# Moving a bias add and PSUM evacuation from TensorE and ScalarE to VectorE, and splitting and merging transposing DMAs, in a linear-attention and ternary-FFN block

## The chip, the cores and the metric

One Trainium2 chip, eight cores. Each core runs the same program on one of eight sequences; nothing is exchanged between them. The metric is the device time of the slowest core in microseconds (us).

## The reference

Per sequence `x` is 4096 x 1024, float32. Attention is linear: no 4096 x 4096 matrix is formed.

```python
h   = layernorm(x)
qkv = h @ Wqkv + bqkv                  # 1024 -> 3072
q, k, v = split(qkv)
q = q / norm(q);  k = k / norm(k)
kv = sum over all rows of (k * v)      # one row of 1024
x = x + (q * kv) @ Wout + bout
h = layernorm(layernorm(x)) * g1 + b1l
h = gelu(h @ ternary(w1).T + b1)       # 1024 -> 4096
h = layernorm(h) * g2 + b2l
x = x + h @ ternary(w2).T + b2         # 4096 -> 1024
# ternary(w) = clip(round(w / m), -1, 1) * m,  m = mean |w|
```

`kv` needs every row before the first output row can be made, so the kernel has two stages.

## The kernel before

The engines' programs are written out by hand, each in one function (`sync`, `scalar`, `gpsimd`, `tensor`, `vector`), and meet only in semaphores. The order of work on an engine is the order of the code, and an instruction that waits holds up all that stands behind it on its engine. A tile is 128 rows; there are NT = 32 tiles.

**First stage** (`for j in range(NT)` in `scalar` and `vector`). SyncE loads tile j of x (L292). ScalarE and VectorE take sum and sum of squares together (`scA_front` L341, `dvA_front` L781); ScalarE writes the normalised tile in bf16 (L353) and stores it to DRAM (L358). SyncE reads it back transposed, eight DMAs of 128 x 128 a tile (`h1t_tile`, L281), into `h1T`, one tile later in the loop. TensorE computes qkv of a tile in six groups of 512 columns. Each group is one float32 matmul over a single row of ones, which puts the bias `rowsA` into the bank (L577, two instructions), and eight bf16 matmuls (L581). The groups take four PSUM banks `pq` in turn, so group i waits until group i-4 has been copied out.

Three tiles behind, `scA_back(u)` (L361) on ScalarE copies the six banks to `qkvb` (L370), squares and sums q and k (L373, L378), and writes `qhat` (L386, stored to DRAM at L390) and `khat` (L395). VectorE (`dvA_back`, L811) gives the two reciprocals (L814, L817), multiplies khat by v (L820) and adds to `kv_acc` (L823).

Beside this the weights w1 and w2 are read by GpSimd through a ring of five slots `wstg` (L539): first VectorE sums their absolute values, six blocks a tile (L770, in tiles 0 to 10 of the loop), then, from u = 10 to u = 25, ScalarE takes two signs of each of four blocks a tile (L427, L429, behind `khat`), VectorE adds them (L778), and GpSimd stores them (L528, L532).

**Between the stages** every engine meets at a barrier; the ternary weights are read back transposed (L308: 4096 rows each, L314: 1024 rows each), scaled and summed.

**Second stage** (pairs of tiles, `for p in range(NT // 2)`). TensorE: `attn_mm(t)` multiplies the transposed q, held in one buffer `qT`, with the scaled Wout (L660). SyncE fills `qT` with eight transposing DMAs a tile (L325), after `attn_mm` of the tile before has ended (semaphore `batt`). `dv_front` and `sc_front` normalise the sum (L935 to L964, L455 to L470), TensorE transposes it (L699), multiplies with w1 for two tiles at once (L719), ScalarE applies Gelu (L493), TensorE multiplies with w2 (L678), and `dv_tail` and `sc_tail` finish and store the tile (L1020 to L1028, L480). In a pair p with tiles j0 and j1, ScalarE runs: `sc_front(j0 + 2)`, 32 Gelus, `sc_tail(j0)`, `sc_front(j1 + 2)`, `sc_tail(j1)`. The w1 matmuls use two PSUM banks, so the third group waits for the first Gelu.

Of the kernel before, what the change touches and what calls it, by code (L numbers as in the profile page):

```python
# [9 lines left out]
F32 = mybir.dt.float32  # L10
BF16 = mybir.dt.bfloat16
AF = mybir.ActivationFunctionType
ALU = mybir.AluOpType
# [42 lines left out]
def build_program(T):  # L56
# [95 lines left out]
    wqkvp = sbA("wqkvp", [128, 8 * E3], BF16)  # L152
    xbufA = sbA("xbufA", [128, 2 * D], F32)
# [114 lines left out]
    with es, esB, psB, nc.Block() as block:  # L268

        @block.sync  # L270
        def _(sy):
            def h1t_tile(jt):
                gt = jt // 4
                st = jt % 4
                sy.wait_ge(ah1w.h(jt % 2), 16 * (jt // 2 + 1))
                if jt >= 4:
                    sy.wait_ge(ah1t.h(jt % 4), 128 * (jt // 4))
                if gt >= 2 and st == 0:
                    sy.wait_ge(aqkv.h, 24 * (gt - 1))
                for c in range(8):  # L280
                    ah1t.inc(sy.dma_start(  # L281
                        out=h1T[:, (gt % 2) * 4096 + c * 512 + st * 128:
                                (gt % 2) * 4096 + c * 512 + (st + 1) * 128],
                        in_=h1_d[jt * 128:(jt + 1) * 128, c * 128:(c + 1) * 128],
                        transpose=True), jt)

            for g in range(NG):
                for s in range(4):
# [6 lines left out]
                    if j - 2 >= 0:  # L295
                        h1t_tile(j - 2)
            for jt in (4 * NG - 2, 4 * NG - 1):
                h1t_tile(jt)
# [18 lines left out]
            for j in range(NT):  # L317
# [4 lines left out]
                if j >= 1:  # L322
                    sy.wait_ge(batt.h, 2 * j)
                for c in range(8):
                    bqt.inc(sy.dma_start(  # L325
                        out=qT[:, c * 128:(c + 1) * 128],
                        in_=qh_d[j * 128:(j + 1) * 128, c * 128:(c + 1) * 128],
                        transpose=True), 16)
# [3 lines left out]
        def _(sc):  # L332
# [28 lines left out]
            def scA_back(u):  # L361
                P = (u % 2) * 16
                if u >= 1:
                    sc.wait_ge(akv.h, u)
                for e in range(6):
                    i = u * 6 + e
                    sc.wait_ge(aqkv.h, i + 1)
                    if e == 0 and u >= 1:
                        sc.wait_ge(aqh.h, u)
                    aevac.inc(sc.activation(out=qkvb[:, e * 512:(e + 1) * 512],  # L370
                                            in_=pq[i % 4][:, :], func=AF.Copy))
                sc.drain()
# [4 lines left out]
                                      in_=stA[:, P + 8:P + 9], func=AF.Sqrt))  # L377
                sc.activation(out=sqscrA[:, :], in_=qkvb[:, D:2 * D],  # L378
# [70 lines left out]

            def sc_front(t):  # L450
# [31 lines left out]

# [645 lines left out]
```

## Time and profile before

| | us |
|---|---|
| median of two runs | 2851.97 |
| the two runs | 2849.68, 2854.25 |
| the profiled execution | 2851.01 |
| its span on the slowest core (core 5) | 2849.4 |
| spans of the eight cores | 2828.0 to 2849.4 |
| mean granted TensorE clock, core 5 | 0.825 of full |
| TensorE / VectorE / ScalarE busy over the span | 67% / 31% / 31% |

The span runs from the first to the last instruction of a core. Busy shares are means over two stages that differ much, so they are of little use alone; the stages are read apart. The granted clock is the share of full speed that the chip allowed TensorE; it moves between 0.5 (1.2 GHz) and 1.0 (2.4 GHz).

### The profile page before, as it was taken

How to read it: one execution, taken by the hardware profiler on the slowest of the kernel's cores; microseconds unless marked ns; L12 is line 12 of the kernel's file. 1: busy time of each engine (PE TensorE's matmuls, PEld its weight loads, DVE VectorE, ACT ScalarE, POOL GpSimd, SP SyncE). 2: the span in 40 equal slices, each digit the busy share in tenths (PEclk: the TensorE clock that was granted, in tenths of full speed). 3: DMA queues.
4: the chain of work that ended last, by engine and by line, in shares of the span. 5: the costliest groups of instructions: out<-in, count | busy, mean ns of one | idle time of the engine just before them, and what ended most of it. 6: DMA issues, size and time to landing. Idle time of an engine off the chain costs nothing.

```text
span 2849.4 us, 36124 instructions; the slowest of 8 cores (2828.0 to 2849.4 us)
## 1 busy us (share of the span) xinstructions
PE 1910.8 (67%) x11300; PEld 960.2 (34%) x11300; DVE 889.3 (31%) x2504; ACT 874.0 (31%) x1505; POOL 118.0 (4%) x217
## 2 busy tenths in 40 slices
PE   0467786666566691457767867686776678677767
PEld 0122221222122230215534544453454345344434
DVE  0533322222222211232253234224323522433343
ACT  0233345655555441002312221321222132212311
POOL 2110001111111000000000000000000000000000
PEclk9977787777766695568889989888998889899889
DMA  9854324444434306700010010001001000100000
GB/s 134 236 166 139 131 67 130 126 129 129 137 123 122 92 30 121 137 23 19 31 38 20 23 34 25 27 26 37 20 23 34 29 28 22 35 20 23 27 16 16
DMA packets 203597, 195.44 MB, mean 69 GB/s; under 512 B 160404, under 2 KB 160405, under 8 KB 203415
## 3 DMA queue, kind: packets, MB, share of 16 engines
q0 software_dynamic: 31200, 92.34, 11.9%
q1 hardware_dynamic: 157952, 67.18, 10.0%
q10 hardware_dynamic: 14264, 33.62, 3.2%
q8 instruction: 100, 1.64, 0.2%
q14 instruction: 81, 0.66, 0.1%
HBM read 117.55 MB, written 50.33 MB: 59 GB/s over the span
## 4 chain that ended last, share of the span: by engine, by line
PE 50%; DVE 12%; ACT 11%; issue 8%; DVEq 7%; DMA 5%; SPq 4%; ACTq 2%; POOL 1%; POOLq 0%
PE py L678 17%; PE py L719 16%; PE pqkv L581 7%; PE pqkv L577 4%; DMA wstg<-w 4%; PE patt L660 2%; DVEq L936 2%; DVEq L790 2%; SPq L314 2%; DVE wpart L770 2%; SPq L308 1%; DVE z1T L1036 1%; DVE outbuf L1020 1%; DVEq L1027 1%; DVE xring L941 1%
## 5 line engine op out<-in xcount | busy, mean ns | idle before, releaser
L678 PE MATMUL py<-w2p,h4buf 128*128 128x512 bf16 x2048 | 541.6, 399 | 124.9 <-DVE outbuf L1028 123.7
L719 PE MATMUL py<-z1T,w1p 128*128 128x256 bf16 x4096 | 481.8, 281 | 165.4 <-ACT h4buf L493 163.6
L577 PE MATMUL pqkv<-rowsA,onesrow 1*128 1x512 f32 x384 | 263.9, 772 | 363.1 <-ACT qkvb L370 284.5
L719 PEld LDWEIGHTS py<-z1T,w1p 128*128 128x128 bf16 x4096 | 382.9, 100 | 264.9 <-issue 170.6
L581 PE MATMUL pqkv<-wqkvp,h1T 128*128 128x512 bf16 x1536 | 448.9, 445 | 0.0
L978 DVE TENSOR_TENSOR h4sq<-h4buf 128x128 bf16<-128x128 bf16 x1024 | 223.3, 225 | 292.5 <-PE psumSQ L687 259.9
L493 ACT ACTIVATE h4buf<-py,beta1c 128x256 bf16<-128x256 f32 x512 | 241.1, 474 | 229.8 <-PE py L719 229.1
L581 PEld LDWEIGHTS pqkv<-wqkvp,h1T 128*128 128x128 bf16 x1536 | 151.6, 109 | 367.4 <-issue 267.5
L1036 DVE CAST z1T<-pzT 128x128 bf16<-128x128 f32 x256 | 56.6, 284 | 580.7 <-PE pzT L699 580.7
L687 PE MATMUL psumSQ<-onesb,h4sq 128*128 128x1 bf16 x1024 | 167.4, 163 | 85.3 <-DVE h4sq L978 85.3
L577 PEld LDWEIGHTS pqkv<-rowsA,onesrow 1*128 1x128 f32 x384 | 68.3, 221 | 462.5 <-issue 462.5
L370 ACT ACTIVATE qkvb<-pqkv 128x512 f32<-128x512 f32 x192 | 104.6, 600 | 274.5 <-PE pqkv L581 246.6
L687 PEld LDWEIGHTS psumSQ<-onesb,h4sq 128*128 128x128 bf16 x1024 | 102.8, 100 | 227.1 <-issue 118.3
L684 PE MATMUL psumSQ<-onesb,h4buf 128*128 128x1 bf16 x1024 | 173.4, 169 | 0.0
L678 PEld LDWEIGHTS py<-w2p,h4buf 128*128 128x128 bf16 x2048 | 125.1, 96 | 128.8 <-issue 127.9
L814 DVE RECIPROCAL stA<-stA 128x1 f32<-128x1 f32 x32 | 5.3, 164 | 463.4 <-ACT stA L376 463.4
L684 PEld LDWEIGHTS psumSQ<-onesb,h4buf 128*128 128x128 bf16 x1024 | 103.3, 101 | 138.2 <-issue 27.8
L455 ACT ACTIVATE xbufB<-xring 128x512 f32<-128x512 f32 x32 | 20.1, 629 | 401.2 <-DVE xring L941 401.2
L660 PE MATMUL patt<-woutp,qT 128*128 128x512 bf16 x512 | 122.3, 394 | 15.9 <-DMA qT<-qhscr 15.9
L477 ACT ACT_TABLE_LOAD x16 | 20.5, 1283 | 355.4 <-DVE stB L1005 355.4
L477 ACT ACTIVATE stB<-stB 128x1 f32<-128x1 f32 x32 | 6.5, 203 | 327.1 <-DVE stB L1005 327.0
L539 POOL DMA_DIRECT2D wstg<-w x128 | 67.7, 530 | 275.1 <-DVE wpart L770 274.3
(124 smaller groups left out, 1370.7 us busy)
## 6 DMA issues: line engine op xcount, KB each, us to landing
wstg<-w POOLq DMA_DIRECT2D x128, 512.0 KB, 5.7
xbufA<-x SPq DMA_DIRECT2D x32, 512.0 KB, 5.2
xbufB<-x SPq DMA_DIRECT2D x32, 512.0 KB, 3.5
out<-outbuf ACTq DMA_DIRECT2D x32, 512.0 KB, 2.7
h1scr<-h1buf ACTq DMA_DIRECT2D x32, 256.0 KB, 5.4
qhscr<-qhat ACTq DMA_DIRECT2D x32, 256.0 KB, 2.0
wqkvp<-wqkv POOLq DMA_DIRECT2D x8, 768.0 KB, 26.1
h1T<-h1scr SPq DMA_TRANSPOSE x256, 2.4
```

Source lines behind the costliest of these rows:

```text
L370: aevac.inc(sc.activation(out=qkvb[:, e * 512:(e + 1) * 512], in_=pq[i % 4][:, :], func=AF.Copy))
L493: bh4.inc(sc.activation(out=h4buf[:, m * 256:(m + 1) * 256], in_=py1[m % 2][:, :], func=AF.Gelu, bias=beta1c[:, m:m + 1]))
L539: wld.inc(gp.dma_start(out=wslot(i), in_=w_src(kind, ch)), i)
L577: te.matmul(out=pq[i % 4][:, :], lhsT=onesrow[:, :], rhs=rowsA[0:1, e * 512:(e + 1) * 512], start=True, stop=False)
L581: mm = te.matmul(out=pq[i % 4][:, :], lhsT=h1T[:, (g % 2) * 4096 + c * 512 + s * 128: (g % 2) * 4096 + c * 512 + (s + 1) * 128], rhs=wqkvp ...
L660: mm = te.matmul(out=patt[:, hh * 512:(hh + 1) * 512], lhsT=qT[:, c * 128:(c + 1) * 128], rhs=woutp[:, c * D + hh * 512:c * D + (hh + 1) * ...
L678: mm = te.matmul(out=py2[:, hh * 512:(hh + 1) * 512], lhsT=h4m, rhs=w2p[:, m * D + hh * 512:m * D + (hh + 1) * 512], start=(m == 0), stop= ...
L684: te.matmul(out=psumSQ[:, m:m + 1], lhsT=h4m, rhs=onesb[:, :], start=True, stop=True)
L687: bsq4.inc(te.matmul(out=psumSQ[:, 32 + m:33 + m], lhsT=h4sq[:, (m % 4) * 128:(m % 4 + 1) * 128], rhs=onesb[:, :], start=True, stop=True))
L719: mm = te.matmul(out=py1[m % 2][:, :], lhsT=w1p[:, c * H + m * 128:c * H + (m + 1) * 128], rhs=z1T[:, c * 256:(c + 1) * 256], start=(c == ...
L978: bsq.inc(dv.tensor_tensor(out=h4sq[:, (m % 4) * 128:(m % 4 + 1) * 128], in0=h4m, in1=h4m, op=ALU.mult))
L1036: cp = dv.tensor_copy(out=z1T[:, c * 256 + (t % 2) * 128:c * 256 + (t % 2) * 128 + 128], in_=pzT[:, cc * 128:(cc + 1) * 128])
```

## The change

It has four parts.

- The bias is added elsewhere. The 192 bias matmuls in the loop go. Before the loop TensorE broadcasts the bias once over 128 partitions, in six pieces through two banks, and VectorE copies it to a new tensor `bqkvb`.
- The six copies out of PSUM go from ScalarE to VectorE, as additions of the bank and `bqkvb`, ahead of the reciprocals in `dvA_back`. ScalarE squares q once two of them are done, and k once four are.
- `h1T` is filled two tiles at a time, with eight DMAs of 256 x 128 in the odd iterations, instead of eight of 128 x 128 in each.
- The `qT` transposes of the odd tiles are issued by ScalarE (`qt_issue`) and no longer by SyncE: that of tile 1 ahead of the second stage's loop, that of tile j1 + 2 at the head of pair p.

```diff
+    bqkvb = sbA("bqkvb", [128, E3], F32)
...
-            def h1t_tile(jt):
+            def h1t_half(jt):
                 gt = jt // 4
                 st = jt % 4
-                sy.wait_ge(ah1w.h(jt % 2), 16 * (jt // 2 + 1))
-                if jt >= 4:
-                    sy.wait_ge(ah1t.h(jt % 4), 128 * (jt // 4))
+                hg = jt // 2
+                sy.wait_ge(ah1w.h(0), 16 * (jt // 2 + 1))
+                sy.wait_ge(ah1w.h(1), 16 * (jt // 2 + 1))
+                if hg >= 4:
+                    sy.wait_ge(ah1t.h(hg % 4), 128 * (hg // 4))
                 if gt >= 2 and st == 0:
                     sy.wait_ge(aqkv.h, 24 * (gt - 1))
                 for c in range(8):
                     ah1t.inc(sy.dma_start(
                         out=h1T[:, (gt % 2) * 4096 + c * 512 + st * 128:
-                                (gt % 2) * 4096 + c * 512 + (st + 1) * 128],
-                        in_=h1_d[jt * 128:(jt + 1) * 128, c * 128:(c + 1) * 128],
-                        transpose=True), jt)
+                                (gt % 2) * 4096 + c * 512 + (st + 2) * 128],
+                        in_=h1_d[jt * 128:(jt + 2) * 128, c * 128:(c + 1) * 128],
+                        transpose=True), hg)
...
-                    if j - 2 >= 0:
-                        h1t_tile(j - 2)
-            for jt in (4 * NG - 2, 4 * NG - 1):
-                h1t_tile(jt)
+                    if j >= 3 and j % 2 == 1:
+                        h1t_half(j - 3)
+            h1t_half(4 * NG - 2)
...
-                if j >= 1:
-                    sy.wait_ge(batt.h, 2 * j)
-                for c in range(8):
-                    bqt.inc(sy.dma_start(
-                        out=qT[:, c * 128:(c + 1) * 128],
-                        in_=qh_d[j * 128:(j + 1) * 128, c * 128:(c + 1) * 128],
-                        transpose=True), 16)
+                if j % 2 == 0:
+                    if j >= 1:
+                        sy.wait_ge(batt.h, 2 * j)
+                    for c in range(8):
+                        bqt.inc(sy.dma_start(
+                            out=qT[:, c * 128:(c + 1) * 128],
+                            in_=qh_d[j * 128:(j + 1) * 128, c * 128:(c + 1) * 128],
+                            transpose=True), 16)
...
             def scA_back(u):
                 P = (u % 2) * 16
-                if u >= 1:
-                    sc.wait_ge(akv.h, u)
-                for e in range(6):
-                    i = u * 6 + e
-                    sc.wait_ge(aqkv.h, i + 1)
-                    if e == 0 and u >= 1:
-                        sc.wait_ge(aqh.h, u)
-                    aevac.inc(sc.activation(out=qkvb[:, e * 512:(e + 1) * 512],
-                                            in_=pq[i % 4][:, :], func=AF.Copy))
-                sc.drain()
+                sc.wait_ge(aevac.h, 6 * u + 2)
                 sc.activation(out=sqscrA[:, :], in_=qkvb[:, 0:D], func=AF.Square,
                               accum_out=stA[:, P + 8:P + 9])
                 sc.drain()
                 aqs.inc(sc.activation(out=stA[:, P + 9:P + 10],
                                       in_=stA[:, P + 8:P + 9], func=AF.Sqrt))
+                sc.wait_ge(aevac.h, 6 * u + 4)
                 sc.activation(out=sqscrA[:, :], in_=qkvb[:, D:2 * D],
                               func=AF.Square, accum_out=stA[:, P + 10:P + 11])
...
+            def qt_issue(t):
+                sc.wait_ge(batt.h, 2 * t)
+                for c in range(8):
+                    bqt.inc(sc.dma_start(
+                        out=qT[:, c * 128:(c + 1) * 128],
+                        in_=qh_d[t * 128:(t + 1) * 128, c * 128:(c + 1) * 128],
+                        transpose=True), 16)
...
+            qt_issue(1)
             sc_front(0)
             sc_front(1)
             for p in range(NT // 2):
                 j0, j1 = 2 * p, 2 * p + 1
+                if j1 + 2 < NT:
+                    qt_issue(j1 + 2)
                 if j0 + 2 < NT:
                     sc_front(j0 + 2)
...
+            for e in range(6):
+                if e >= 2:
+                    te.wait_ge(binit.h, e - 1)
+                abc.inc(te.matmul(out=pq[e % 2][:, :], lhsT=onesrow[:, :],
+                                  rhs=rowsA[0:1, e * 512:(e + 1) * 512],
+                                  start=True, stop=True))
             for hh in range(2):
+                te.wait_ge(binit.h, 5 + hh)
...
-            te.wait_ge(binit.h, 2)
+            te.wait_ge(binit.h, 8)
...
-                    te.wait_ge(ah1t.h(s), 128 * (g + 1))
+                    hg = 2 * g + s // 2
+                    te.wait_ge(ah1t.h(hg % 4), 128 * (hg // 4 + 1))
                     for e in range(6):
                         i = (4 * g + s) * 6 + e
                         if i >= 4:
                             te.wait_ge(aevac.h, i - 3)
-                        te.matmul(out=pq[i % 4][:, :], lhsT=onesrow[:, :],
-                                  rhs=rowsA[0:1, e * 512:(e + 1) * 512],
-                                  start=True, stop=False)
...
-                                start=False, stop=(c == 7))
+                                start=(c == 0), stop=(c == 7))
...
+            for e in range(6):
+                dv.wait_ge(abc.h, e + 1)
+                binit.inc(dv.tensor_copy(out=bqkvb[:, e * 512:(e + 1) * 512],
+                                         in_=pq[e % 2][:, :]))
...
             def dvA_back(u):
                 P = (u % 2) * 16
+                for e in range(6):
+                    i = u * 6 + e
+                    dv.wait_ge(aqkv.h, i + 1)
+                    if e == 0 and u >= 1:
+                        dv.wait_ge(aqh.h, u)
+                    if e == 2 and u >= 1:
+                        dv.wait_ge(akh.h, u)
+                    aevac.inc(dv.tensor_tensor(
+                        out=qkvb[:, e * 512:(e + 1) * 512],
+                        in0=pq[i % 4][:, :],
+                        in1=bqkvb[:, e * 512:(e + 1) * 512], op=ALU.add))
                 dv.wait_ge(aqs.h, u + 1)
```

Unchanged: what is computed, the order of tiles, the weights' path, and the second stage but for who issues the odd `qT`.

VectorE in the first stage, one tile of the part that makes ternary weights; before:

```order
L808 TENSOR_TENSOR stA<-stA 128x1
L814 RECIPROCAL stA<-stA 128x1
L817 RECIPROCAL stA<-stA 128x1
L820 TENSOR_TENSOR kvtmp<-khat,qkvb 128x1024
L823 TENSOR_TENSOR kv_acc<-kv_acc,kvtmp 128x1024
L778 TENSOR_TENSOR qod<-qod,qog 128x1024 x2
L778 TENSOR_TENSOR qtd<-qtd,qtg 128x1024 x2
L788 TENSOR_REDUCE stA<-xbufA 128x1
L791 TENSOR_SCALAR stA<-stA 128x1
```

and after:

```order
L823 TENSOR_TENSOR stA<-stA 128x1
L835 TENSOR_TENSOR qkvb<-pqkv,bqkvb 128x512 x6
L840 RECIPROCAL stA<-stA 128x1
L843 RECIPROCAL stA<-stA 128x1
L846 TENSOR_TENSOR kvtmp<-khat,qkvb 128x1024
L849 TENSOR_TENSOR kv_acc<-kv_acc,kvtmp 128x1024
L793 TENSOR_TENSOR qod<-qod,qog 128x1024 x2
L793 TENSOR_TENSOR qtd<-qtd,qtg 128x1024 x2
L803 TENSOR_REDUCE stA<-xbufA 128x1
L806 TENSOR_SCALAR stA<-stA 128x1
```

Six additions from the banks `pqkv` now stand between the last small operation of the front (a row that writes `stA`) and the two reciprocals; the signs' sums (`qod`, `qtd`) and the next tile's `TENSOR_REDUCE` stay behind `kv_acc`.

ScalarE in the second stage, from the end of one pair to the first Gelus of the next (`out` is the store of a finished tile, the operations on `xbufB` are the squares of `sc_front`); before:

```order
L477 ACTIVATE stB<-stB 128x1
L480 DMA out<-outbuf 128x1024
L455 ACTIVATE xbufB,stB<-xring 128x512
L457 ACTIVATE xbufB,stB<-xring 128x512
L460 ACTIVATE stB<-stB 128x1
L465 ACTIVATE stB<-stB 128x1
L470 ACTIVATE z1buf<-xring,stB 128x1024
L493 ACTIVATE h4buf<-py_0,beta1c 128x256
```

and after:

```order
L480 ACTIVATE stB<-stB 128x1
L483 DMA out<-outbuf 128x1024
L448 DMA_TRANSPOSE qT<-qhscr 128x128 x8
L458 ACTIVATE xbufB,stB<-xring 128x512
L460 ACTIVATE xbufB,stB<-xring 128x512
L463 ACTIVATE stB<-stB 128x1
L468 ACTIVATE stB<-stB 128x1
L473 ACTIVATE z1buf<-xring,stB 128x1024
L499 ACTIVATE h4buf<-py_0,beta1c 128x256
```

Eight transposing DMAs now stand between the store and the squares of the next front.

## Rows read from the trace of the kernel before

**Rows 1.** Windows of core 5: us, busy (x) of each engine, PEclk, DMA share, GB/s.

```profile
412.00:970.00 558.00, 359.68 (x964) 113.87 (x964) 120.75 (x246) 315.96 (x417) 66.93 (x125) 0.72 0.41 125
1241.00:2849.00 1608.00, 1165.51 (x8961) 712.73 (x8960) 578.76 (x1922) 386.99 (x800) 0.00 (x0) 0.87 0.09 26
```

**Rows 2.** Timeline of ScalarE at four tiles: start, us, engine, line, form.

```profile
119.54 1.24 ACT L353 ACTIVATE h1buf<-xbufA,stA 128x1024 bf16<-128x1024 f32 x1 [0.65 <-DVE stA L808]
...
362.62 1.24 ACT L353 ACTIVATE h1buf<-xbufA,stA 128x1024 bf16<-128x1024 f32 x1 [0.65 <-DVE stA L808]
...
411.79 1.24 ACT L353 ACTIVATE h1buf<-xbufA,stA 128x1024 bf16<-128x1024 f32 x1 [0.65 <-DVE stA L808]
...
969.83 1.24 ACT L353 ACTIVATE h1buf<-xbufA,stA 128x1024 bf16<-128x1024 f32 x1 [0.65 <-DVE stA L808]
```

**Rows 3.** The line of the last accumulation: ns min/median/max, first and last start.

```profile
L823 DVE TENSOR_TENSOR kv_acc<-kv_acc,kvtmp x32: 1225/1226/1226, 137.1 to 1086.5; 128x1024 f32<-128x1024 f32 x32
```

**Rows 4.** Timeline, 548 to 584 us: one tile of the ternary stretch.

```profile
548.17 2.07 ACT L370 ACTIVATE qkvb<-pqkv 128x512 f32<-128x512 f32 x4 [0.66 <-ACT h1buf L353]
...
548.91 2.04 PE L577 MATMUL pqkv<-rowsA,onesrow 1*128 1x512 f32 x2 [12.17 <-ACT qkvb L370]
550.88 3.59 PE L581 MATMUL pqkv<-wqkvp,h1T 128*128 128x512 bf16 x8
...
554.57 0.60 ACT L370 ACTIVATE qkvb<-pqkv 128x512 f32<-128x512 f32 x1 [4.34 <-PE pqkv L581]
...
560.10 0.60 ACT L370 ACTIVATE qkvb<-pqkv 128x512 f32<-128x512 f32 x1 [4.93 <-PE pqkv L581]
...
563.93 1.90 PE L581 MATMUL pqkv<-wqkvp,h1T 128*128 128x512 bf16 x8
...
565.17 1.15 ACT L395 ACTIVATE khat<-qkvb,stA 128x1024 f32<-128x1024 f32 x1 [0.57 <-ACT qhat L386]
...
578.06 1.21 DVE L788 TENSOR_REDUCE stA<-xbufA 128x1 f32<-128x1024 f32 x1
...
580.71 0.16 DVE L808 TENSOR_TENSOR stA<-stA 128x1 f32<-128x1 f32 x1
...
582.92 1.57 ACT L370 ACTIVATE qkvb<-pqkv 128x512 f32<-128x512 f32 x3 [0.66 <-ACT h1buf L353]
```

**Rows 5.** Timeline, 195 to 232 us: one tile of the stretch that sums weights.

```profile
200.12 6.84 DVE L770 TENSOR_REDUCE wpart<-wstg 128x1 f32<-128x1024 f32 x6
...
206.87 1.22 DVE L788 TENSOR_REDUCE stA<-xbufA 128x1 f32<-128x1024 f32 x1
...
211.74 2.06 ACT L370 ACTIVATE qkvb<-pqkv 128x512 f32<-128x512 f32 x4 [0.66 <-ACT h1buf L353]
...
221.40 0.60 ACT L370 ACTIVATE qkvb<-pqkv 128x512 f32<-128x512 f32 x1 [2.66 <-PE pqkv L581]
```

**Rows 6.** Timeline, 22 to 77 us: the bias of the output projection at the start.

```profile
22.35 3.75 PE L565 MATMUL pqkv<-boutrow,onesrow 1*128 1x512 f32 x4 [22.35 <-DMA identb<-ident_d]
...
75.43 1.28 DVE L748 COPY boutb<-pqkv 128x512 f32<-128x512 f32 x2
```

**Rows 7.** Timeline, 1677 to 1690 us: the start of a pair in the second stage.

```profile
1677.32 9.92 SPq L325 DMA_TRANSPOSE qT<-qhscr  x8
...
1680.51 0.34 ACTq L480 DMA_DIRECT2D out<-outbuf  x1
...
1683.16 0.63 ACT L455 ACTIVATE xbufB<-xring 128x512 f32<-128x512 f32 x1 [7.22 <-DVE xring L941]
...
1689.71 3.57 PE L719 MATMUL py<-z1T,w1p 128*128 128x256 bf16 x16 [10.71 <-ACT h4buf L493]
```

**Rows 8.** Three DMA issuing lines: ns min/median/max, first and last start.

```profile
L314 SPq DMA_TRANSPOSE w2p<-wq2scr x32: 1144/1273/3143, 1138.8 to 1185.1; - x32
L325 SPq DMA_TRANSPOSE qT<-qhscr x256: 1085/1202/2376, 1187.0 to 2676.0; - x128
L390 ACTq DMA_DIRECT2D qhscr<-qhat x32: 338/338/367, 134.1 to 1083.5; - x32
```

More of the change, by code:

```diff
@@ L745, in _ @@
                                       scalar1=0.5, scalar2=None, op0=ALU.mult))
+            for e in range(6):
+                dv.wait_ge(abc.h, e + 1)
+                binit.inc(dv.tensor_copy(out=bqkvb[:, e * 512:(e + 1) * 512],
+                                         in_=pq[e % 2][:, :]))
             for hh in range(2):
-                dv.wait_ge(abc.h, hh + 1)
+                dv.wait_ge(abc.h, 7 + hh)
                 binit.inc(dv.tensor_copy(out=boutb[:, hh * 512:(hh + 1) * 512],
@@ L1069, in build_program @@
         "mpre": 2, "mtot": 2, "mval": 2, "mbc": 2, "m1r": 1, "m2r": 1,
-        "abc": 2, "binit": 2, "kvc": 8, "kvw": 1, "bar": 5,
+        "abc": 8, "binit": 8, "kvc": 8, "kvw": 1, "bar": 5,
         "w1t": 128, "w2t": 512,
@@ L1080, in build_program @@
     }
-    dexpect = {"ax": 16 * NT, "ah1w": 16 * NT, "ah1t": 512 * NG,
+    dexpect = {"ax": 16 * NT, "ah1w": 16 * NT, "ah1t": 64 * NT,
                "aqw": 16 * NT, "wld": 16 * NLOADS,
```

## The prediction

> **What bounds the kernel now.** I read the stages apart: first the windows, then the timeline of single tiles inside them. TensorE is granted 0.72 of its clock and works 359.68 of 558 us in the stretch that makes ternary weights, and 1165.51 of 1608 us in the second stage [rows 1]. So it bounds neither stage alone: something makes it wait once a tile and once a pair, and the chain through that wait sets the time.
>
> In the first stage the start of `h1buf` on ScalarE marks the tiles. From 119.54 to 362.62 eight intervals sum weights (30.4 us each), two up to 411.79 do neither (24.6 us), sixteen up to 969.83 make ternary weights (34.9 us), and the last accumulation starts at 1086.5 and ends 1.2 later [rows 2, 3], 117.9 us after 969.83. One tile of the ternary stretch shows the loop [rows 4]. ScalarE copies four banks at 548.17 that had long been full. TensorE waited 12.17 us for the first of them, and then does two groups at the low clock, 2.04 of bias and about 3.5 of real work each. ScalarE waits 4.34 and 4.93 us for them and ends its sixth copy at 560.70. Only then come the squares, qhat and khat (to 566.32), eight signs, and the next front. The loop is ScalarE and VectorE in series with two groups of TensorE, nothing of which overlaps.
>
> The second stage's 1608 us hold 16 pairs, about 100 each [rows 1]. At its start TensorE has two w1 groups done and waits 10.71 us for the first Gelu, which stands behind `sc_front` on ScalarE [rows 7]. `sc_front` itself starts at 1683.16, after VectorE has finished the old tile and made the new sum. The transposes of the odd q tile run meanwhile on SyncE, from 1677.32 for 9.92 us, and hold nobody up.
>
> **First stage, the loop.** I count from r, the start of VectorE's reduction of the front. Before, the ternary tile's r is 578.06, its first copy starts at r + 4.9 and ends its sixth 12.5 later (560.70 less 548.17), at r + 17.4; khat ends 5.6 after that, at r + 23.0 [rows 4]. After, VectorE is free when the front's last operation ends, at 580.87, r + 2.8, and need not wait for h1buf. One addition of 128 x 512 float32 out of PSUM isn't in the trace. Half of one of 128 x 1024 is 0.61 us [rows 3], and the copies of a bank at the start take 0.64 each [rows 6]; I take 0.65, nearer to the row with PSUM (both ends together move a tile by 0.1). The first ends at r + 3.55 and frees TensorE. Its group is now only the eight matmuls, 3.59 us at the low clock [rows 4], so the fifth group ends at r + 7.1 and the sixth, if still slow, at r + 10.7; the sixth addition ends at r + 11.4. The squares run on ScalarE under this. VectorE's reciprocals stand behind all six additions: the new wait costs ScalarE some 3 us of idleness ahead of qhat. After 0.35 us for both, qhat, the issue of its store and khat take 1.15 + 0.57 + 1.15, and khat ends at r + 14.6. That is 8.4 earlier. The rest of the tile stays as it is, signs included. The ring of weights must turn faster; at a DMA share of 0.41 [rows 1] I give back 0.3. **Sixteen tiles by 8.1: -130 us.** If the sixth group runs at the high clock (1.90 [rows 4]) it is 27 us more.
>
> For the tiles that sum weights r is 206.87, the first copy starts at r + 4.9 and the sixth ends at 222.0, r + 15.1, with khat 5.6 on at r + 20.7 [rows 5]. There only one group ran slow. New: 3.55 + 3.59 + 1.90 + 0.65 = r + 9.7, khat at r + 12.9, 7.8 earlier. The six sums of 6.84 us [rows 5] then ask for six blocks in about 23 us instead of 30, so I give back 0.8. **Eight tiles by 7.0: -56.** The two tiles without weights end at khat's 12.9 plus two operations of 1.23 [rows 3], near 16 each instead of 24.6: **-17.** From 969.83 on there are two such intervals (32), a back alone (13), and three tiles without a front. Those three were TensorE's: six groups with their bias. Now six by 1.90 is 11.4, and I take 12 each. 32 + 13 + 36 = 81 against 117.9: **-37.**
>
> The removed bias matmuls are thus worth 2 us a slow group where VectorE waits for it, and the moved copies the time that ScalarE stood behind h1buf and its store. I don't add TensorE's whole bias time, since most of it lay in the shade of the signs.
>
> **Merged transposes.** A DMA of 1024 rows occupies SyncE 1273 ns, one of 128 rows 1202 [rows 8], so one of 256 costs about 1.2, and SyncE issues half as many. But SyncE is not in the loop: gain nothing. An even tile's `h1T` now comes with the odd one: behind the odd tile's h1buf lie its store, eight issues of 1.2, 9.6 us, and two landings. TensorE asks for it one interval later plus two groups, near 20 us even at 16 us a tile. The cover is thin in the short tiles, and worth 2 to 4 us each if gone. At the very start it makes TensorE's first group later by about one interval of the start and its eight issues, of which nearly all lies beside the first three fronts.
>
> **Start.** Six more banks are broadcast and copied. VectorE reaches them only at 75.43 [rows 6]. Two are ready by then; six more follow at 1.9 each (half of 3.75 [rows 6]), about 12 us on VectorE's path. The transfers that keep VectorE waiting afterwards get ahead meanwhile, so from 0 to 14 I take **+10**, near the upper end, as the later h1T is in it.
>
> **Second stage.** The eight issues stand on ScalarE now, behind the store (issued at 1680.51, done at 1680.85 [rows 7]) and before `sc_front`. Behind them are queued the squares, the root, z1buf, and all 32 Gelus; VectorE waits for the squares and TensorE for the Gelus. The trace has no transpose on ScalarE. SyncE's row has 1202 ns each, 9.92 us for eight; a plain store issued on ScalarE has 338 ns, so eight would be 2.7 [rows 7, 8]. Those are the ends, and I take 9.92, the same operation on the same kind of queue. `sc_front` then starts at 1690.8 instead of 1683.16, 7.6 later; at the lower end 0.4. The wait for `attn_mm` (done at 1677.3) is over before. All of it is on the path, since TensorE already waits for that very Gelu and has nothing else in its program. No gain stands against it, since SyncE's transposes were hidden. Fourteen pairs by 7.6 and the first, where no store or tail hides anything, by 8.6: **+115 us.** The last pair has none.
>
> The Trainium skill (DMA: Bandwidth & Descriptors, "Issuing engines are not separate DMA queues") says that spreading DMAs over engines saves only the sequencer's issue time, usually small beside the transfer. Taken as a price for ScalarE, that would make this part nearly free; the 1202 ns of the row speak against it here, and no run yet shows it on ScalarE. The same skill (TensorE: Matmul & The Clock Gate, on queue depths) calls ScalarE's queue strictly first in, first out, which is why I let the Gelus wait.
>
> **Sum.** -130 - 56 - 17 - 37 + 10 + 115 = -115. The profiled execution took 2851.0 us, span 2849.4; that gives 2736. The median of the runs is 1 us above the profiled one: **2737 us.**
>
> **Rivals.**
> - *Issuing a transpose on ScalarE is as cheap as a store.* Then the second stage loses 0.4 by 15, 6 us and not 115: 2737 - 109 = 2628. For it: the stores' 338 ns. Against: the same operation's 1202 on SyncE. This is also where the page's rule leads. Chance 0.08.
> - *Half of the loop's gain goes into a new wait*: the ring of weights or a late `h1T` becomes what ends last. For it: the DMA share of 0.41, and bursts of six blocks through five slots. Half of 240 is 120: 2857. Chance 0.13.
> - *The weight stream paces the stage wholly.* If GpSimd's ring cannot turn faster than 30.4 and 34.9 us, the 24 weight tiles gain nothing. What is left is -54, against +125: 2923, slower. It decides where those tiles gain less than 3.0 us each (71 by 24). Against: [rows 5] shows six blocks consumed in 6.84 us with no gap, so they had landed early. Chance 0.06.
> - *TensorE's clock.* Its wait per pair grows from 10.7 to 18.3 us. After 10.71 the first sixteen w1 matmuls take 3.57 instead of about 1.9 [rows 7]. If a longer wait left the clock low for one more such stretch, 1.7 to 3.5 us by 15 would be added: 2763 to 2790. It lies inside the forecast's case.
>
> **How the numbers follow.** The forecast's case gets 0.73. Its own range is 2680 to 2795: down by the fast sixth group (27), issues of 1.085 (17) and a free start (10), up by the clock (52) and the start. A measurement of this kernel tells about 2%, 57 us, from no change. Faster by more than that (under 2795) are the forecast's case and the first rival: 0.80. Within 2% is mostly the second: 0.14. Slower by over 2% is the third: 0.06. The range leaves out most of the first and third and part of the second: 2665 to 2840.
>
> **What would show it.** Right: no `rowsA` matmul in the loop; additions near 0.65; h1buf intervals of about 23, 16 and 27 us; ScalarE idle before qhat for VectorE's reciprocal; an ACTq row of eight transposes near 9.8 us at the head of each pair, and TensorE idle some 18 us before the w1 matmuls, in pairs 7 to 8 us longer. Wrong: transposes of 0.35 on ScalarE, or squares that start beside them; intervals above 30 with VectorE or ScalarE waiting for `wstg`; TensorE waiting for `h1T`.

## The result, and the profile after

The changed kernel takes 2781.32 us (median of 11 runs, 2773.42 to 2787.67), in a ratio of 0.973 to the kernel before run beside it (ten runs, median 2857.46), 95% interval 0.9701 to 0.9759: faster by 2.7%. Here and below medians are over all runs of a kernel and ratios are not: in some runs the cores of one die show a lower clock and a longer span, and those stand outside the ratios. The profiled execution took 2781.41, its span on core 6 is 2779.9 against 2849.4 before. The direction and the range held; the point, 2737, was 44 us low.

The end of the first stage (the last accumulation) parts the span in two. Before it comes at 1087.7 us, now at 864.7. What follows took 1761.7 us and now takes 1915.1. So the first stage gave 223.0 us and the second took 153.4 back.

The marks of the first stage, that answer to [rows 2, 3]: the starts of `h1buf` on ScalarE in tiles 3, 11, 13 and 29 (columns: start, us, engine, line, form), in the changed kernel.

```profile
132.44 1.24 ACT L356 ACTIVATE h1buf<-xbufA,stA 128x1024 bf16<-128x1024 f32 x1 [0.65 <-DVE stA L823]
...
335.10 1.24 ACT L356 ACTIVATE h1buf<-xbufA,stA 128x1024 bf16<-128x1024 f32 x1 [0.65 <-DVE stA L823]
...
367.82 1.24 ACT L356 ACTIVATE h1buf<-xbufA,stA 128x1024 bf16<-128x1024 f32 x1 [0.65 <-DVE stA L823]
...
788.32 1.24 ACT L356 ACTIVATE h1buf<-xbufA,stA 128x1024 bf16<-128x1024 f32 x1 [0.65 <-DVE stA L823]
```

And the line of `kv_acc`, whose last instruction ends the stage (duration ns min/median/max, first and last start):

```profile
L849 DVE TENSOR_TENSOR kv_acc<-kv_acc,kvtmp x32: 1224/1226/1226, 159.4 to 863.5; 128x1024 f32<-128x1024 f32 x32
```

The sixteen ternary tiles now take 26.3 us each, (788.32 - 367.82) / 16, instead of 34.9. One of them, answering to [rows 4], in the timeline of the changed kernel:

```profile
495.54 1.21 DVE L803 TENSOR_REDUCE stA<-xbufA 128x1 f32<-128x1024 f32 x1
...
498.72 2.48 DVE L835 TENSOR_TENSOR qkvb<-pqkv,bqkvb 128x512 f32<-128x512 f32 x4
498.86 1.24 ACT L356 ACTIVATE h1buf<-xbufA,stA 128x1024 bf16<-128x1024 f32 x1 [0.65 <-DVE stA L823]
499.56 5.86 PE L592 MATMUL pqkv<-wqkvp,h1T 128*128 128x512 bf16 x16 [13.78 <-DVE qkvb L835]
...
503.24 0.69 DVE L835 TENSOR_TENSOR qkvb<-pqkv,bqkvb 128x512 f32<-128x512 f32 x1 [2.03 <-PE pqkv L592]
...
505.52 0.69 DVE L835 TENSOR_TENSOR qkvb<-pqkv,bqkvb 128x512 f32<-128x512 f32 x1 [1.59 <-PE pqkv L592]
...
506.44 1.15 ACT L381 ACTIVATE qhat<-qkvb,stA 128x1024 bf16<-128x1024 f32 x1 [3.06 <-DVE stA L840]
508.16 1.15 ACT L390 ACTIVATE khat<-qkvb,stA 128x1024 f32<-128x1024 f32 x1 [0.57 <-ACT qhat L381]
...
520.83 1.21 DVE L803 TENSOR_REDUCE stA<-xbufA 128x1 f32<-128x1024 f32 x1
```

Counted from r, the start of VectorE's `TENSOR_REDUCE`, its additions start at r + 3.2 (498.72 less 495.54), beside ScalarE's h1buf and no longer behind it. TensorE's two groups take 5.86 us together and not 11 (the granted clock is 0.50 up to 503.20 and 0.80 in the 2.3 us after it, so the second group is partly fast). The sixth addition ends at r + 10.7. ScalarE then has waited 3.06 us for the reciprocal, and khat ends at r + 13.8; before it was r + 23.0.

At the head of a pair of the second stage, answering to [rows 7]:

```profile
1607.81 0.34 ACTq L483 DMA_DIRECT2D out<-outbuf  x1
1608.23 10.29 ACTq L448 DMA_TRANSPOSE qT<-qhscr  x8
...
1618.62 0.63 ACT L458 ACTIVATE xbufB<-xring 128x512 f32<-128x512 f32 x1 [15.38 <-issue]
...
1625.17 7.02 PE L730 MATMUL py<-z1T,w1p 128*128 128x256 bf16 x39 [18.88 <-ACT h4buf L499]
```

(The last row counts only what had started when the window asked for ended.) The eight issues hold ScalarE for 10.29 us. The first square starts 10.81 us after the store, where it was 2.65 (1683.16 less 1680.51). TensorE waits 18.88 us, where it was 10.71. The pairs, from first Gelu to first Gelu, take 109.2 us in the mean of fourteen and not 99.0.

Behind the wait TensorE runs slower too. Two groups by line (busy us, mean ns of one, idle before and its releaser), first of the kernel before, then of the changed one:

```profile
L678 PE MATMUL py<-w2p,h4buf 128*128 128x512 bf16 x2048 | 541.6, 399 | 124.9 <-DVE outbuf L1028 123.7
L719 PE MATMUL py<-z1T,w1p 128*128 128x256 bf16 x4096 | 481.8, 281 | 165.4 <-ACT h4buf L493 163.6 <-DVE z1T L1036 1.4
```

```profile
L689 PE MATMUL py<-w2p,h4buf 128*128 128x512 bf16 x2048 | 560.0, 409 | 125.4 <-DVE outbuf L1054 124.2 <-issue 0.2
L730 PE MATMUL py<-z1T,w1p 128*128 128x256 bf16 x4096 | 494.1, 286 | 287.3 <-ACT h4buf L499 285.8 <-DVE z1T L1062 1.4
```

The same 2048 and 4096 matmuls take 30.7 us more (560.0 + 494.1 against 541.6 + 481.8), 2.0 a pair, and the wait for the Gelu 122.2 us more (285.8 against 163.6), 8.1 in each of fifteen pairs. Together 152.9 of the 153.4 us, 10.2 a pair.

### The profile page after: what moved, and what is told of

The parts are those of the page before. It is cut to its first block, busy times and chain, and to the rows that moved or that the text cites. A ratio compares the mean times of both kernels' runs of the same rounds, so it can differ in the third digit from the quotient of the medians.

```text
span 2779.9 us, 35286 instructions; the slowest of 8 cores (2757.0 to 2779.9 us)
## 1 busy us (share of the span) xinstructions
PE 1660.3 (60%) x10928; PEld 917.9 (33%) x10928; DVE 1011.1 (36%) x2702; ACT 771.0 (28%) x1313; POOL 118.0 (4%) x217
## 4 chain that ended last, share of the span: by engine, by line
PE 48%; DVE 12%; issue 9%; ACT 8%; ACTq 7%; DMA 6%; DVEq 6%; SPq 4%; POOL 1%; POOLq 0%
PE py L689 18%; PE py L730 17%; PE pqkv L592 7%; ACTq L448 6%; DMA wstg<-w 4%; PE patt L671 2%; DVEq L805 2%; SPq L316 2%; DVE z1T L1062 1%; SPq L310 1%; DVE outbuf L1046 1%; DVEq L1053 1%; DVE kvtmp L846 1%; ACT qhat L381 1%; ACT khat L390 1%
## 5 line engine op out<-in xcount | busy, mean ns | idle before, releaser
L730 PE MATMUL py<-z1T,w1p 128*128 128x256 bf16 x4096 | 494.1, 286 | 287.3 <-ACT h4buf L499 285.8
L689 PE MATMUL py<-w2p,h4buf 128*128 128x512 bf16 x2048 | 560.0, 409 | 125.4 <-DVE outbuf L1054 124.2
L592 PE MATMUL pqkv<-wqkvp,h1T 128*128 128x512 bf16 x1536 | 397.7, 426 | 371.5 <-DVE qkvb L835 318.3
L730 PEld LDWEIGHTS py<-z1T,w1p 128*128 128x128 bf16 x4096 | 390.4, 102 | 391.6 <-issue 292.0
L592 PEld LDWEIGHTS pqkv<-wqkvp,h1T 128*128 128x128 bf16 x1536 | 162.1, 107 | 606.3 <-issue 468.2
L835 DVE TENSOR_TENSOR qkvb<-pqkv,bqkvb 128x512 f32<-128x512 f32 x192 | 124.1, 687 | 120.5 <-PE pqkv L592 119.7
L785 DVE TENSOR_REDUCE wpart<-wstg 128x1 f32<-128x1024 f32 x64 | 74.5, 1214 | 16.7 <-DMA wstg<-w 16.4
L671 PEld LDWEIGHTS patt<-woutp,qT 128*128 128x128 bf16 x512 | 50.4, 101 | 75.0 <-issue 24.2
L846 DVE TENSOR_TENSOR kvtmp<-khat,qkvb 128x1024 f32<-128x1024 f32 x32 | 39.2, 1226 | 98.7 <-ACT khat L390 98.7
```

The lines of the kernel that those rows point to most:

```text
L592: mm = te.matmul(out=pq[i % 4][:, :], lhsT=h1T[:, (g % 2) * 4096 + c * 512 + s * 128: (g % 2) * 4096 + c * 512 + (s + 1) * 128], rhs=wqkvp ...
L671: mm = te.matmul(out=patt[:, hh * 512:(hh + 1) * 512], lhsT=qT[:, c * 128:(c + 1) * 128], rhs=woutp[:, c * D + hh * 512:c * D + (hh + 1) * ...
L689: mm = te.matmul(out=py2[:, hh * 512:(hh + 1) * 512], lhsT=h4m, rhs=w2p[:, m * D + hh * 512:m * D + (hh + 1) * 512], start=(m == 0), stop= ...
L730: mm = te.matmul(out=py1[m % 2][:, :], lhsT=w1p[:, c * H + m * 128:c * H + (m + 1) * 128], rhs=z1T[:, c * 256:(c + 1) * 256], start=(c == ...
L785: dcons.inc(dv.tensor_reduce(out=wpart[:, col:col + 1], in_=wslot(i), axis=AX.X, op=ALU.add, apply_absolute_value=True))
L835: aevac.inc(dv.tensor_tensor(out=qkvb[:, e * 512:(e + 1) * 512], in0=pq[i % 4][:, :], in1=bqkvb[:, e * 512:(e + 1) * 512], op=ALU.add))
```

## The experiments

Every run is compared with runs of the kernel before on its own chip; those had medians of 2863, 2865 and 2856 us in the three groups (e1 to e4, e5 to e8, f1 to f3), so across groups only ratios are set side by side. "End of first stage" is the end of the last accumulation, on the slowest core.

### e1: all qT transposes back on SyncE

```diff
-                if j % 2 == 0:
-                    if j >= 1:
-                        sy.wait_ge(batt.h, 2 * j)
...
+                if j >= 1:
+                    sy.wait_ge(batt.h, 2 * j)
...
-            qt_issue(1)
...
-                if j1 + 2 < NT:
-                    qt_issue(j1 + 2)
```

> The changed kernel with all qT transposes back on SyncE. Theory: the eight issues on ScalarE are the whole loss of the second stage, in two parts: the wait for the first Gelu (7.4 us a pair) and about 2.8 us a pair of low TensorE clock behind it. Without them the pair returns from 109.2 to 99.0 us, and the kernel comes to 2781 - 15 x 10.2 = 2628 us. Rival: the longer pairs belong to the clock after another first stage, or to the loads of x; then only the 15 x 7.4 of the wait comes back: 2670 us, with pairs near 102.

2640.7 us, ratio 0.9205 (0.9153 to 0.9258). Pairs are 99.0 us again, and what follows the first stage takes 1765.7. The matmuls behind the wait are back too:

```profile
L677 PE MATMUL py<-w2p,h4buf 128*128 128x512 bf16 x2048 | 542.1, 399 | 125.5 <-DVE outbuf L1042 124.2 <-issue 0.2
L718 PE MATMUL py<-z1T,w1p 128*128 128x256 bf16 x4096 | 481.9, 281 | 164.8 <-ACT h4buf L487 163.1 <-DVE z1T L1050 1.3
```

542.1 and 481.9 are the numbers of before. So both the wait and the slow matmuls hang on the moved issues, and the one edit costs 0.973 - 0.9205 of the time before, 5.3% or 150 us. The theory's 2628 was reckoned from the first runs, beside which the kernel before took 2857 us; here it takes 2863.

### e2: only the moved qT transposes

```diff
 (kernel before)
+                if j % 2 == 0:
+                    if j >= 1:
+                        sy.wait_ge(batt.h, 2 * j)
...
+            qt_issue(1)
...
+                if j1 + 2 < NT:
+                    qt_issue(j1 + 2)
```

> The kernel before with only the odd qT transposes moved to ScalarE. Theory: plus 15 x 10.2 = 153 us, so about 3005 us, pairs of 109.2 us, first stage as before. Rival (parts depend on each other): under 2980, or a first stage that changes too.

3017.3 us, ratio 1.0515 (1.0459 to 1.0571), pairs of 109.2; the first stage ends at 1096.5, with ternary tiles of 34.7. The loss is the same beside the old first stage, 5.2%: the parts add up.

### e3: only the bias and PSUM part

```diff
 (changed kernel, h1t_tile and qT on SyncE as before)
```

> The kernel before with only the bias and PSUM part: neither the merged transposes nor the moved qT. Theory: the whole gain of the first stage is here, and the merged transposes only cost: their even tile comes late at the start. First h1T at about 115 us instead of 141, and 10 to 15 us faster than the kernel with all qT on SyncE: about 2615 us. Rival: the merged transposes relieve SyncE and the DMA queues and carry a part of the gain; then this is slower than that kernel, above 2635.

2635.0 us, ratio 0.9175 (0.9097 to 0.9253). The first stage ends at 871.9, ternary tiles take 27.3, and TensorE's first group starts at 120.5 us. The whole gain is in this part. That it is also faster than e1 by the cost of the merged transposes isn't settled: 0.9175 and 0.9205 lie inside each other's intervals.

### e4: only the merged h1T transposes

```diff
 (kernel before)
-                    if j - 2 >= 0:
-                        h1t_tile(j - 2)
+                    if j >= 3 and j % 2 == 1:
+                        h1t_half(j - 3)
...
```

> The kernel before with only the merged h1T transposes. Theory: SyncE isn't in the loop, so nothing is gained; the first tile is late and costs 5 to 15 us once: 2857 to 2867 us. Rival: half as many transposes free DMA time for the weights: 10 us or more faster than before, under 2842.

2877.3 us, ratio 1.0044 (1.0018 to 1.0071): 13 us slower. The first wait of TensorE shows it, from the waits of this run and of the one before it (engine, line, releaser: us, times, longest):

```profile
PE pqkv L579 <- DMA h1T<-h1scr: 106.2, 1, 106.2
```

```profile
PE pqkv L578 <- DMA h1T<-h1scr: 30.6, 1, 30.6
```

The first tile's `h1T` is waited for 106.2 us, against 78.5 in the kernel before; in e3 it is 30.6 after the bias broadcasts. So the wait is 28 us longer, of which 13 reach the end. Ternary tiles are as long as before (34.9). The merging gains nothing, and what it costs arises at the start.

### e5: the bias matmuls back on TensorE

```diff
+                        te.matmul(out=pq[i % 4][:, :], lhsT=onesrow[:, :],
+                                  rhs=rowsA[0:1, e * 512:(e + 1) * 512],
+                                  start=True, stop=False)
...
-                    aevac.inc(dv.tensor_tensor(
+                    aevac.inc(dv.tensor_copy(
```

> The run with the bias and PSUM part alone, but the bias matmuls put back in front of each group and VectorE only copying the bank (the broadcast before the loop stays). It parts the two gains. Theory: of the ternary tile's 7.6 us the bias's share is the two slow groups, 2 x 2.0 us, and the move's share 3.5 to 4: tiles of 31 us in the ternary stretch, 26 in the sums', and the last tiles back at 17.3; in all about 16 x 3.8 + 8 x 3 + 2 x 3 + 25 = 115 us slower than that run, near 2750. Rival: only the move counts, since the matmuls lie in the shade of the signs: under 2680.

2764.5 us, ratio 0.9631 (0.9589 to 0.9673), so beside e3 (0.9175, with an interval of 0.8% to either side) the bias matmuls are worth some 4.6% and the move alone 3.7%. The first stage ends at 993.0. Ternary tiles take 30.8 us, tiles that sum weights 26.8, those with neither 20.8, and from tile 29 to the end 104.8 instead of 75.2. Two slow groups of one tile, from its timeline:

```profile
578.01 2.04 PE L577 MATMUL pqkv<-rowsA,onesrow 1*128 1x512 f32 x2 [7.63 <-DVE qkvb L824]
...
579.98 3.59 PE L581 MATMUL pqkv<-wqkvp,h1T 128*128 128x512 bf16 x8
...
583.50 2.07 PE L577 MATMUL pqkv<-rowsA,onesrow 1*128 1x512 f32 x2
...
585.51 3.59 PE L581 MATMUL pqkv<-wqkvp,h1T 128*128 128x512 bf16 x8
...
589.21 0.69 DVE L824 COPY qkvb<-pqkv 128x512 f32<-128x512 f32 x1 [4.83 <-PE pqkv L581]
```

Each group has 2.0 us of bias in front of VectorE's copy. The gain is thus about half one and half the other in the ternary tiles (34.9, 30.8, 27.3), and two thirds bias from tile 29 on (29.6 of 42.7 us).

### e6: the reciprocals ahead of the sixth addition

```diff
+                    if e == 4:
+                        dv.wait_ge(aqs.h, u + 1)
+                        aqr.inc(dv.reciprocal(...))
+                        dv.wait_ge(aks.h, u + 1)
+                        akr.inc(dv.reciprocal(...))
+                dv.wait_ge(aevac.h, 6 * (u + 1))
```

> The run with the bias and PSUM part alone, with both reciprocals ahead of the sixth addition. Theory: ScalarE's wait before qhat (2 to 3 us in the trace) is the place of the reciprocals in VectorE's program; qhat and khat move up by one group of TensorE and an addition (2.4 to 3.6 us), so tiles with signs are 2.5 to 3 us shorter, those that end on VectorE 1 to 1.5: about 55 us faster, 2580. Rival: the gain goes into a wait for the weights' landings or the sixth group: under 20 us.

2565.0 us, ratio 0.8941 (0.8903 to 0.8979), 2.3% less than e3's. Ternary tiles are 24.8 us, those that sum weights 21.6, those with neither 13.4. ScalarE's wait before qhat, in the waits of e3 and of this run:

```profile
ACT qhat L379 <- DVE stA L826: 92.9, 32, 3.8
```

```profile
ACT qhat L379 <- DVE stA L827: 20.7, 29, 1.1
```

92.9 us became 20.7. The place of two operations of 0.15 us behind an addition that waits for TensorE had cost 1.8 to 3.1 us in each tile.

### e7: TensorE kept busy in the wait, in the changed kernel

```diff
+                    if m == 2:
+                        for _ in range(150):
+                            te.matmul(out=pzT[:, 0:256], lhsT=w1p[:, 0:128],
+                                      rhs=z1T[:, 0:256], start=True, stop=True)
```

> The changed kernel with 150 additional 256-column matmuls into a free bank while TensorE waits for the first Gelu of a pair (extra work whose result nobody reads). Theory: the 2.8 us a pair beyond the wait are the clock, which falls in a wait of 19 us and costs again behind it. With the array busy it stays at full: pairs of 104.5 to 106.5 us instead of 109.2, 40 to 70 us faster, 2711 to 2741. Rival: the clock isn't the cause, or falls elsewhere: pairs of 109 or more.

2778.3 us, ratio 0.9683 (0.9651 to 0.9715), against 0.973 (0.9701 to 0.9759): not told apart. Pairs scatter from 105.2 to 109.3 us, 107.7 in the mean where they were 109.2, and the mean granted clock rose from 0.807 to 0.858 on the slowest core. The expected 104.5 to 106.5 was missed, but not because the clock doesn't matter:

```profile
L689 PE MATMUL py<-w2p,h4buf 128*128 128x512 bf16 x2048 | 551.7, 404 | 125.1 <-DVE outbuf L1058 124.3
L734 PE MATMUL py<-z1T,w1p 128*128 128x256 bf16 x4096 | 469.1, 277 | 44.4 <-ACT h4buf L499 42.9 <-DVE z1T L1066 1.4
L729 PE MATMUL pzT<-z1T,w1p 128*128 128x256 bf16 x2400 | 265.3, 273 | 0.0
```

The real matmuls take 33.3 us less than in the changed kernel (551.7 + 469.1 against 560.0 + 494.1). The added ones and what is left of the wait take 22.4 more than the wait did (265.3 + 42.9 against 285.8); the last pair has no long wait to fill, and from its first Gelu to the end takes 88.3 us and not 78.2. Behind the first stage this profile has 1893.3 us where the changed kernel has 1915.1; its first stage, which the edit doesn't touch, was longer (to 885.7 and not 864.7). So most of what filling gave back it also cost.

### e8: eight plain stores in place of the transposes

```diff
 (e1's kernel)
+                sc.wait_ge(batt.h, 2 * t)
+                for c in range(8):
+                    bdum.inc(sc.dma_start(out=dum_d[c * 128:(c + 1) * 128, :],
+                                          in_=boutb[:, 0:1]), 16)
```

> The changed kernel with all qT transposes on SyncE, and at the place on ScalarE where the odd ones stood eight plain stores of 512 bytes each to a scratch tensor. It prices the rival of my prediction. Theory: the cost is the time that an issue holds ScalarE. Eight plain ones are 8 x 0.34 = 2.7 us, of which all but 0.4 lies beside VectorE's own chain: pairs of 99.0 to 99.6, within 10 us of the run without them (2641). Rival: any eight DMAs there cost the same as transposes: pairs of 106 or more.

2706.93 us in the one run that could be compared; no ratio was worked out. The profile is of another (2753.6), and the timeline is of core 4, whose span is 2680.9 us, the shortest there:

```profile
1368.58 0.35 ACTq L483 DMA_DIRECT2D out<-outbuf  x1
1369.02 4.78 ACTq L449 DMA_DIRECT2D dumscr<-boutb  x8
...
1373.89 0.63 ACT L458 ACTIVATE xbufB<-xring 128x512 f32<-128x512 f32 x1 [9.88 <-issue]
...
1380.44 19.73 PE L730 MATMUL py<-z1T,w1p 128*128 128x256 bf16 x159 [13.29 <-ACT h4buf L498]
```

A store of 128 pieces of 4 bytes holds ScalarE 0.60 us here (4.78 / 8; the median of all is 0.57), not the 0.34 that I had from stores of whole tiles. The first square comes 5.31 us after the store instead of 2.65, and TensorE waits 13.29 us instead of 10.71: each kind of issue costs its own time, and what VectorE's chain doesn't cover is passed on whole (2.66 and 2.58 us). Neither number expected was right (99 to 99.6, or 106); core 4's first ten pairs are 101.5 to 103.4, and 2.6 of the 3.6 us by which its pairs grew in the mean are that wait.

### f1: the transposes one at a time between the Gelus

```diff
 (e3's kernel; SyncE issues the even tiles only)
+                    if j1 + 2 < NT and m % 3 == 2 and m // 3 < 8:
+                        qt_one(j1 + 2, m // 3)
```

> The run with the bias and PSUM part alone, and the odd qT transposes on ScalarE again, but one after every third Gelu instead of eight in a row ahead of the front. Theory: an issue holds ScalarE 1.27 us and the next Gelu has 0.40 us of slack (0.875 a group of TensorE, 0.47 a Gelu) and only two banks, so each issue costs at most 0.87 us: 3 to 7 us a pair instead of 10.2, pairs of 102 to 106, 50 to 110 us slower than the run without (2635 beside 2863). Rival: ScalarE is idle 45% of the time among the Gelus and the issues vanish there: pairs of 99 to 100, under 15 us.

2681.0 us, ratio 0.9383 (0.935 to 0.9417), against e3's 0.9175: 2.1% slower, 60 us. Pairs are 102.4 (e3: 99.0). The issuing line, and TensorE's wait for Gelus:

```profile
L447 ACTq DMA_TRANSPOSE qT<-qhscr x128: 1094/1097/1870, 1021.8 to 2521.9; - x128
```

```profile
PE py L729 <- ACT h4buf L497: 186.3, 120, 11.0
```

Here an issue takes 1097 ns, and 120 waits stand where there were 16, so nearly every issue makes one. ScalarE has idle time enough in the sum, but in pieces of 0.40 us between two Gelus, and two banks let TensorE run no further ahead. The waits for Gelus grew by only 23.2 us, though (186.3, e3 163.1); TensorE's w1 and w2 lines are 14.8 and 12.1 us longer (496.6 and 554.2, e3 481.8 and 542.1), and why isn't settled.

### f2: the bias broadcast before the wait for the constants

```diff
-            dv.wait_ge(gmld.h, 16 * 5)
 (and the two operations on b1lc and b2lc: now behind the loop)
```

> The run with the early reciprocals, and VectorE's wait for the small constants of the second stage moved from the head of its program to behind the loop. It tests the cost of the start: the bias copies then run at 25 to 37 us, when VectorE waits anyway, and not after 75. Theory: the 12 us of the copies go and the first front starts under 40 us, but TensorE still needs Wqkv and the sums the weights' landings: first accumulation 15 to 30 us earlier, 2565 -> 2535 to 2550 beside 2865. Rival: the loads of Wqkv set the start anyway: under 5 us.

2539.0 us, ratio 0.8892 (0.8864 to 0.892), against e6's 0.8941. The first accumulation starts at 130.5 instead of 149.2. VectorE at the start, from its timeline:

```profile
37.02 1.21 DVE L784 TENSOR_REDUCE stA<-xbufA 128x1 f32<-128x1024 f32 x1
...
79.61 1.22 DVE L766 TENSOR_REDUCE wpart<-wstg 128x1 f32<-128x1024 f32 x1 [39.77 <-DMA wstg<-w]
```

The first front is 53 us earlier (in e6 it starts at 90.07), but the sums then wait 39.8 us for the first weights. 18.7 us of it reach the first accumulation. This is the fastest version of the study by its median: 11.1% under the kernel before.

### f3: f2 with a shorter filling

```diff
+                        for _ in range(70):
```

> The same with 70 additional 256-column matmuls into a free bank while TensorE waits 10.7 us for the first Gelu of a pair (nobody reads their result). Theory: the clock doesn't fall there; 1.7 us or more a pair come back at the first groups: pairs of 96 to 97.5 instead of 99, 25 to 45 us faster than the run without. Rival: as with the 150 before, the low clock moves to another place of the pair: under 10 us.

2547.8 us, ratio 0.8919 (0.8889 to 0.895): no gain over f2. Groups by line, first f2, then f3:

```profile
L716 PE MATMUL py<-z1T,w1p 128*128 128x256 bf16 x4096 | 482.4, 282 | 164.4 <-ACT h4buf L486 162.7 <-DVE z1T L1050 1.4
L675 PE MATMUL py<-w2p,h4buf 128*128 128x512 bf16 x2048 | 542.4, 399 | 125.1 <-DVE outbuf L1042 123.7 <-issue 0.2
```

```profile
L720 PE MATMUL py<-z1T,w1p 128*128 128x256 bf16 x4096 | 477.2, 280 | 44.9 <-ACT h4buf L486 43.1 <-DVE z1T L1054 1.3
L675 PE MATMUL py<-w2p,h4buf 128*128 128x512 bf16 x2048 | 546.3, 402 | 124.7 <-DVE outbuf L1046 123.6
L715 PE MATMUL pzT<-z1T,w1p 128*128 128x256 bf16 x1120 | 125.4, 273 | 0.0
```

The w1 matmuls get 5.2 us faster and the w2 matmuls 3.9 slower; the 70 extra ones with the rest of the wait (125.4 + 43.1) take 5.8 more than the wait they fill (162.7). Pairs stay at 99.0 (f2: 99.1), and the last one is 2 us longer. The filling costs at least what it gives.

## Why the prediction was right, and where it was off

**The loop of the first stage** was right step by step. The terms measured, on the slowest cores: sixteen ternary tiles -137.6 us (said -130), the two without weights -16.5 (-17), from tile 29 on -41.5 (-37). Of the eight tiles that sum weights the first belongs to the start; the other seven gave -7.2 each (-7.0). VectorE was let in before h1buf, its addition takes 0.69 us alone and 0.62 in a row of four (said 0.65), and the new wait before qhat was 3.06 (some 3). e3 shows that all of it is this edit, e5 that the bias matmuls and the move share it, and e6 that the wait was real: with most of it gone a ternary tile is 2.5 us shorter. What I gave back for the weights' landings was about right or small: VectorE waits for `wstg` 16.4 us in all against 11.0, ScalarE 43.9 against 38.3.

**The start** was mis-sized: "+10" was +23 (12.9 to tile 3's h1buf, 10.3 to the next one), and with the gain of the eighth tile that isn't seen there about 30. The copies cost the 12 us that I had reckoned: the changed kernel's timeline shows them from 77.04, with TensorE's broadcasts waiting for VectorE in turn (the row of 7.16 us holds four, two instructions each), and the first h1buf comes 12.5 us later. That a part of this would vanish beside the transfers did not come true.

```profile
77.04 1.28 DVE L759 COPY bqkvb<-pqkv 128x512 f32<-128x512 f32 x2
77.87 7.16 PE L573 MATMUL pqkv<-rowsA,onesrow 1*128 1x512 f32 x8 [50.70 <-DVE bqkvb L759]
...
141.69 19.41 PE L592 MATMUL pqkv<-wqkvp,h1T 128*128 128x512 bf16 x80 [53.24 <-DMA h1T<-h1scr]
```

What failed besides is that the late `h1T` "lies beside the first three fronts". TensorE's first group starts at 141.69, after tile 3's h1buf at 132.44 (before, it started at 104.64, and in e3 at 120.52), and VectorE has nothing to add until then. e4 prices this at 0.44%, 13 us, where I had said gain nothing.

That the first stage came out at -223 beside a forecast of -230 is thus partly luck: the loop gave some 13 us more than I said (253 with the eighth tile, against 240), and the start took 20 more.

**The second stage** had the right mechanism and too small a size: +153.4 where I said +115. Two pieces make the difference. The squares come 8.2 us later, not 7.6 (10.81 less 2.65): a transpose is issued on ScalarE in 1266 ns (1202 on SyncE), by its line in the changed kernel.

```profile
L448 ACTq DMA_TRANSPOSE qT<-qhscr x128: 1110/1266/1282, 1027.6 to 2600.3; - x128
```

The other 2.0 us a pair are TensorE's matmuls at the low clock. I had this as a rival inside the range, at 1.7 to 3.5 a pair, and left it out of the sum. The larger half isn't where I put it, behind the wait. The w1 matmuls behind the wait take 12.3 us more and the w2 matmuls 18.4. A part of those lies at the start of a tile's w2 matmuls, where two of them take 1.01 us and not 0.59 (granted clock 0.50 from 1661.3 to 1663.9, 1.00 from 1664.8 to 1677.0; at the same place in the kernel before it is 1.00 throughout, 1723.1 to 1739.3):

```profile
1660.75 0.59 PE L689 MATMUL py<-w2p,h4buf 128*128 128x512 bf16 x2
...
1661.23 1.01 PE L689 MATMUL py<-w2p,h4buf 128*128 128x512 bf16 x2
```

e1 takes both pieces away with the issues. e7 shows that the second hangs on the idle wait: with the wait filled the matmuls are 33.3 us faster again, but the filling costs most of that. Why a pair of 109.2 us has this low stretch and one of 99.0 hasn't stays open.

**The rivals.** "As cheap as a store" fell by the row of 1266 ns. The Trainium skill's remark on issuing engines (DMA: Bandwidth & Descriptors, "Issuing engines are not separate DMA queues"), that an issue is usually small beside its transfer, doesn't fit a transpose of 128 x 128 here: 1.27 us to issue, 2.4 us to land, and 150 us for 128 of them ahead of work that TensorE waits for. "Half of the gain goes into a new wait" and "the weight stream paces the stage" fell by the tiles' lengths.

So -70 came of a sum of -115: 38 us of the gap are the second stage, 7 the first.

## What to carry to other kernels

In this kernel a DMA's issue was work of the engine that issues it. Before moving one, multiply its issue row by the count and look at what is queued behind it there; SyncE, otherwise idle, had done the same for nothing, and spreading it between short operations still cost 2.1 of the 5.3%. When an engine takes over work, put what another engine waits for ahead of the instruction that itself has to wait: two 0.15 us operations one place earlier gave 2.3%. And test a bundle of edits apart: here one part gave 8%, one cost 0.4%, and one took 5% back.

## What the runs showed of the hardware

- The time to issue a transpose differed by place: 1266 ns on ScalarE in a row of eight (changed kernel, median), 1202 on SyncE (before), 1097 one at a time among Gelus (f1). Merging two blocks of 128 rows left it at 1242 on SyncE.
- A store of 128 x 4 bytes took longer to issue, 0.57 us in the median (e8, core 4), than one of 128 rows of 2 or 4 KB, 0.34 to 0.37 (kernel before).
- Filling TensorE's wait of 19 us with 150 matmuls raised the mean granted clock from 0.807 to 0.858 and made the real w1 and w2 matmuls 33.3 us faster (e7), but the whole was not measurably faster, since the filling itself took 22.4 us more than the wait: a higher granted clock over the span is not yet a shorter time.
